# A vision block on one core: VectorE takes half of image 0's rotations, and the last steps get an order of their own

## What is computed

```python
h = wavelet_tokens(x, Wa, ba, Wd1, bd1, Wd2, bd2, Wd3, bd3)   # (32, 256, 256)
h = concatenate([cls_tok, h], axis=1)                          # 257 tokens
n = layernorm(h)
q, k, v = split(einsum('bsd,dhf->bshf', n, w_qkv) + b_qkv, 3)  # 16 heads of 64
q, k = q * cos + rotate_half(q) * sin, k * cos + rotate_half(k) * sin
s = q @ k.T / sqrt(192) + alibi, causal
h = h + softmax(s) @ v @ w_out + b_out
n = layernorm(h)                                               # feed-forward: 256 -> 1024 -> 256
h = h + bitlinear(silu(bitlinear(n, w_gate)) * bitlinear(n, w_up), w_down)
```

## Time and profile before

| | us |
|---|---|
| median of 3 runs (1750.04 to 1756.24) | 1754.96 |
| profiled execution | 1752.32 |
| its span, first to last instruction | 1750.50 |
| TensorE busy | 1664.2 |
| VectorE busy | 1470.0 |
| ScalarE busy | 1323.6 |
| POOL busy | 1120.1 |

### The profile page before, as it was taken

How to read it: one execution, slowest core, us unless ns; L and a number is a source line. 1 busy time by engine, 2 the same in 40 slices (tenths; PEclk the granted TensorE clock), 3 DMA queues, 4 the chain that set the end, 5 groups by cost and what they waited for, 6 DMA issues and landing times.

```text
span 1750.5 us, 48653 instructions
## 1 busy us (share of the span) xinstructions
PE 1664.2 (95%) x16742; PEld 1278.3 (73%) x16742; DVE 1470.0 (84%) x4972; ACT 1323.6 (76%) x3812; POOL 1120.1 (64%) x1034
## 2 busy tenths in 40 slices
PE   7758999999999999999999999999999999999975
PEld 6635777777777777777777777777777777777653
DVE  3837888899888888899888888899888888889874
ACT  0326888888888888888888888888888888888762
POOL 0087667766777666766777667666677667666500
PEclk9789999999999999999999999999999999999986
DMA  9311111111111111111111111111111111111100
GB/s 320 110 61 61 56 53 56 53 67 57 61 68 68 59 61 57 50 65 62 56 68 68 66 55 60 54 56 66 55 64 68 68 53 61 56 53 62 44 7 13
DMA packets 90168, 113.70 MB, mean 65 GB/s; under 512 B 14818, under 2 KB 52163, under 8 KB 89667
## 3 DMA queue, kind: packets, MB, share of 16 engines
q1 hardware_dynamic: 89922, 110.59, 18.1%
HBM read 26.62 MB, written 8.42 MB: 20 GB/s over the span
## 4 chain that ended last, share of the span: by engine, by line
PE 88%; DVE 4%; SPq 3%; POOL 2%; ACT 1%; issue 1%; DMA 0%; DVEq 0%; POOLq 0%; ACTq 0%
PE bank L725 45%; PE bank L842 9%; PE bank L983 7%; PE bank L831 6%; PE bank L829 6%; PE bank L994 3%; PE bank L853 3%; PE bank L903 3%; PE bank L891 2%; PE bank L1003 2%; SPq L320 1%; PE bank L882 1%; DVE arena L1283 1%; PE bank L950 0%; POOL rot L486 0%
## 5 line engine op out<-in xcount | busy, mean ns | idle before, releaser
L482 POOL TENSOR_TENSOR arena<-rq,cos 128x512 f32<-128x512 f32 x256 | 326.1, 1274 | 280.0 <-ACT rq L526 280.0
L535 ACT ACTIVATE arena<-arena,nm 128x129 f32<-128x129 f32 (+1 forms) x1024 | 455.6, 455 | 0.0
L486 POOL TENSOR_TENSOR rot<-rot,sin 128x512 f32<-128x512 f32 x256 | 326.3, 1275 | 103.9 <-DMA rot<-rq 103.9
L725 PE MATMUL bank<-xt_h,weights 128*128 128x256 f16 x2048 | 378.9, 273 | 9.2 <-ACT rq L526 7.8
L526 ACT ACTIVATE rq<-bank,bqk 128x256 f32<-128x256 f32 x512 | 214.4, 471 | 170.1 <-PE bank L725 155.3
L1283 DVE CUSTOM_DVE_ANT_0 arena<-bank,bias 128x129 f32<-128x129 f32 (+1 forms) x1024 | 317.9, 352 | 26.5 <-issue 16.6
L489 POOL TENSOR_TENSOR arena<-arena,rot 128x512 f32<-128x512 f32 x256 | 314.2, 1228 | 37.3 <-POOL rot L486 0.9
L1291 DVE TENSOR_TENSOR ptr_l<-bank,ptr_h 128x384 f16<-128x384 f32 x512 | 280.0, 552 | 31.8 <-ACT ptr_h L545 29.4
L545 ACT ACTIVATE ptr_h<-bank 128x384 f16<-128x384 f32 x512 | 249.1, 486 | 68.6 <-PE bank L725 44.0
L725 PE MATMUL bank<-xt_l,weights 128*128 128x256 f16 x1024 | 279.6, 273 | 0.0
L842 PE MATMUL bank<-eye,arena 128*128 128x128 f32 x1536 | 253.0, 277 | 8.5 <-DVE ptr_l L1291 4.4
(11 more groups left out here) (200 smaller groups left out, 3182.5 us busy)
## 6 DMA issues: line engine op xcount, KB each, us to landing
rot<-rq SPq DMA_DIRECT2D x512, 128.0 KB, 2.0
arena<-in_x SPq DMA_DIRECT2D x4, 2048.0 KB, 15.2
xin<-in_x SPq DMA_DIRECT2D x32, 256.0 KB, 2.8
hr<-hr SPq DMA_DIRECT2D x32, 256.0 KB, 2.3
out<-h SPq DMA_DIRECT2D x64, 128.0 KB, 2.1
arena<-in_L_attn_w_qkv SPq DMA_DIRECT2D x2, 1536.0 KB, 8.6
weights<-in_L_ffn_w_down SPq DMA_DIRECT2D x1, 1024.0 KB, 11.8
arena<-in_L_ffn_w_gate SPq DMA_DIRECT2D x1, 1024.0 KB, 8.5
```

What stands on the lines that cost most here:

```text
L482: pool.tensor_tensor(dst, rq[:, g % 2].rearrange("p j (t n) -> p j t n", t=T), cos[:, :].rearrange("p (t n) -> p t n", t=T).unsqueeze(1).b ...
L486: pool.tensor_tensor(r, r, sin[:, :].unsqueeze(1).broadcast_to([P, 2, SIDE]), ALU.mult).then_inc(t2_ready, 1)
L535: act.activation(cols, cols, ACT.Exp, bias=nm[:, t, h:h + 1], scale=-1.0, accum_out=rs[:, t, h:h + 1]).then_inc(e_done, 1)
L725: ins = pe.matmul(dst, lhs[l], rhs[r], start=start and n == 0, stop=stop and n == len(parts) - 1)
```

## The change

In the preparation, rotate(0, 1), rotate(0, 3), rotate(0, 5) and rotate(0, 7) go from POOL to VectorE, with waits that keep the three counters of the rotations in order. POOL does rotate(0, 0) ahead of add_bias(0). VectorE's image_operators(1, 16), image_out(1), image_stats(1), the split of wo_l and image_operators(17, 15) are placed between the rotations. The turns of the ternary weights go behind coarse(0) and between the first projections, on the banks 0, 1, 4 and 6, with their copies on ScalarE; the ternary steps of VectorE are spread accordingly. The mean of the weights is taken inside the last quarter of the gates' product. move(0) also waits until the weights are turned, because hr2 holds the third of them until then.

The loops end with step 29. Steps 30 to 33 (images 29 to 31 and the blocks up to 32) are written out call by call on each engine. The calls are the same; their order differs, on TensorE and ScalarE from step 30, on VectorE from the calls that go with it, on SP in the DMAs of these steps, and on POOL in one exchange, token_rstd(31) ahead of rotate(31, 7).

```diff
 # SP
+                if c == 0:
+                    sp.wait_ge(turned, 6)
 # POOL
-                if not image(b):
+                if not image(b) or begun and (b, g) == (0, 0) or b == 0 and g % 2:
                     return
+                if b == 0 and g:
+                    pool.wait_ge(pcos_done, g)
...
             pool.wait_ge(late_in, 16 * 13)
+            image_rstd(0)
+            rotate(0, 0)
 # ScalarE
+            coarse_out(0)
+            weights_out(0)
+            weights_out(1)
+            input_hi(0)
+            to_rotate(0, 0)
+            to_rotate(0, 1)
+            weights_out(2)
+            weights_out(3)
+            to_rotate(0, 2)
+            weights_out(4)
+            weights_out(5)
             act.wait_ge(rawo_in, 16)
             act.wait_ge(tern_ready, 3)
             act.activation(wo_h[:, :, :], rawo, ACT.Copy, scale=WSCALE).then_inc(w_hi, 1)
 # TensorE
             cls_part(psum[3], (2,), range(PAIRS))
+            pe.wait_ge(mean_ready, 1)
+            turn_weights(0)
             turn_input(0)
...
-            out_bias(range(0, 4))
             project(0, 0)
-            out_bias(range(4, PAIRS))
+            out_bias(range(PAIRS))
             pe.matmul(psum[2][:, 0:SIDE], ones[0:1, :], bo_row, start=False, stop=True).then_inc(ob_ready, 1)
+            project(0, 1)
+            turn_weights(1)
+            project(0, 2)
+            turn_weights(2)
 # VectorE
+            def rotate(b, g):
+                r = rot[:, g % 2].rearrange("p j (t n) -> p j t n", t=T)
+                dst = rope_out(b % 2, GROUPS[g])
+                dve.wait_ge(rq_ready, g + 1)
+                dve.wait_ge(pcos_done, g)
+                tt(dst, rq[:, g % 2]..., cos..., ALU.mult).then_inc(pcos_done, 1)
+                dve.wait_ge(rot_done[g % 2], 32 * (g // 2 + 1))
+                dve.wait_ge(t2_ready, g)
+                tt(rot[:, g % 2], rot[:, g % 2], sin..., ALU.mult).then_inc(t2_ready, 1)
+                dve.wait_ge(pcos_done, g + 1)
+                dve.wait_ge(t2_ready, g + 1)
+                dve.wait_ge(qk_done, g)
+                tt(dst, dst, r, ALU.add).then_inc(qk_done, 1)
...
             normalise_image(0)
-            dve.wait_ge(ops_ready, 1)
-            image_operators(1, 16)
+            ternary(1, 2)
             input_lo(0)
...
+            for part in range(3):
+                ternary(2, part)
+            prep_chain.settle()
+            rotate(0, 1)
             dve.wait_ge(ob_ready, 1)
             dve.tensor_copy(ob[:, :], psum[2][:, 0:SIDE]).then_inc(ob_copied, 1)
+            dve.wait_ge(ops_ready, 1)
+            image_operators(1, 16)
+            rotate(0, 3)
+            image_out(1)
+            image_stats(1)
+            rotate(0, 5)
+            dve.wait_ge(w_hi, 11)
+            stt(wo_l[:, :, :], rawo, WSCALE, wo_h[:, :, :], ALU.mult, ALU.subtract).then_inc(wo_split, 1)
+            rotate(0, 7)
             dve.wait_ge(ops_ready, 2)
             image_operators(17, 15)
```

More of the change, by code:

```diff
@@ L468, in image_rstd @@
             def image_rstd(a):
-                if not image(a):
+                if not image(a) or begun and a == 0:
                     return
@@ new lines, in _ @@
+            values(29, 2)
+            values(29, 3)
+            project(30, 4)
+            coarse(31)
+            synthesise(31)
+            scores(29, 4)
+            turn_tokens(29)
+            transposes(29, 6)
+            values(29, 4)
+            project(30, 5)
+            out_transposes(29, 0)
+            gate_up(29, 0)
+            project(30, 6)
+            values(29, 5)
+            transposes(29, 7)
+            scores(29, 5)
+            transposes(29, 8)
+            gate_up(29, 1)
@@ new lines, in _ @@
+            values(29, 6)
+            project(30, 7)
+            values(29, 7)
+            transposes(29, 9)
+            scores(29, 6)
+            project_v(30, 0)
+            gate_up(29, 2)
+            values(29, 8)
+            transposes(29, 10)
+            out_transposes(29, 1)
+            project_v(30, 1)
+            scores(29, 7)
+            values(29, 9)
+            transposes(29, 11)
+            project_v(30, 2)
+            turn_inner(29, 0)
+            transposes(29, 12)
@@ new lines, in _ @@
+            values(29, 10)
+            transposes(29, 13)
+            values(29, 11)
+            project_v(30, 3)
+            scores(30, 0)
+            gate_up(29, 3)
+            turn_input(31)
+            values(29, 12)
+            values(29, 13)
+            transposes(29, 14)
+            scores(30, 1)
+            out_transposes(29, 2)
+            project(31, 0)
+            down(29, 0)
+            transposes(29, 15)
+            project(31, 1)
+            values(29, 14)
+            transposes(30, 0)
@@ new lines, in _ @@
+            transposes(30, 5)
+            values(30, 3)
+            project(31, 4)
+            scores(30, 3)
+            project(31, 5)
+            turn_tokens(30)
+            scores(30, 4)
+            gate_up(30, 0)
+            values(30, 4)
+            transposes(30, 6)
+            out_transposes(30, 0)
+            scores(30, 5)
+            values(30, 5)
+            values(30, 6)
+            transposes(30, 7)
+            gate_up(30, 1)
+            transposes(30, 8)
+            project(31, 6)
@@ new lines, in _ @@
+            inner_peak(31, 3)
+            weights_lo(31, 13)
+            weights_lo(31, 14)
+            reciprocals(31, 3)
+            attended_lo(31, 2)
+            weights_lo(31, 15)
+            output(31, 0)
+            normalise(31, 3)
+            output(31, 1)
+            attended_lo(31, 3)
+            residual(32)
+            token_scales(32)
+            gate(32, 0)
+            gate_up(32, 0)
+            inner_peak(32, 0)
+            gate(32, 1)
+            gate_up(32, 1)
```

664 lines of the change are left out of this document (633 added, 31 removed).

## The result

| | us |
|---|---|
| before, median of 20 runs (1750.04 to 1756.24) | 1753.23 |
| after, median of 20 runs (1754.56 to 1758.85) | 1756.38 |
| ratio of after to before | 1.0019, interval 1.0012 to 1.0026 (95%) |
| profiled execution of after, its span | 1756.73, 1754.9 |

The time rose by 3.2 us. With so many runs that can be told from nothing, but it is well within the 0.5% that the prediction counts as no change. The total held. Its two large terms did not come out as written: the preparation costs 13 to 15 us and the last steps give back about 10.

A forecast was written before the change was run, and what follows sets the result against it. TensorE fills the steady step, so only start and end can move the time, the start through a chain of waits. Preparation +10.3 and last steps -8.4 give +1.9 on 1754.96, about 1757 us, range 1746 to 1768.

The forecast's parts named there:

- H: End of VectorE's hh in the preparation, 113.9 before; forecast 114.9 with port exclusion, 111.3 without; taken as +0.5 us.
- queue behind H: VectorE work queued ahead of values_lo(0,0), delaying the first value: floor +5.4, with port exclusion +9.65, taken as +8.5 us.
- lower clock behind coarse(1): TensorE idles about 9 us, then three value products run slower at the lower clock: 0 to +4, taken as +1.3 us.
- The exclusion: Preparation: VectorE instructions with two SBUF inputs and POOL's SBUF reads exclude one another; H +1.0 with it, -2.6 without.
- Move(0)'s new wait: Preparation: waiting for turned 6 costs nothing, since add_bias(0), which move(0) awaits too, ends later.
- Turn_tokens(30)'s and turn_inner(31,1)'s waits: Last steps: waits of 1.40 and 3.02 us, shortened by project(31,5) and by a maximum and rounding placed ahead: -1.3 and -3.0.
- The item of turn_tokens(31): Last steps, residual(31) to turn_tokens(31), waits of 2.29 and 1.48: token_scales passes weights_lo(31,4), giving -0.6 us.
- The last block: Block 32: inner_peak(32,2) and a scale, formerly behind gate_up(32,3) on the chain, now lie in a wait: -0.8 us.
- The short waits: Last steps: seven short waits of 5.6 us in all, giving back -1.5 us, a guess.
- the end of step 31: Two waits of 1.04 and 0.92 us, partly filled by project_v(31) stretched out later and scores(31) sooner: -1.2 us.
- the slower one: Port lockstep between H and values_lo(0,0), products at the lower clock: +14, only -3 from the end, 1766 us; chance 0.24.
- The faster one: POOL and VectorE hardly stop one another, or POOL's free time absorbs the late start: 1744.8 us or -8.4; together 0.16.

The follow-up runs named there:

- e4: Changed kernel with wo_l's split ahead of rotate(0,5) and image_operators(17,15) in two halves behind the second and third value products; 1750.43 us, ratio 0.9988 to before.
- e5: Changed kernel with cos and sin copied into a PSUM bank for VectorE's rotations, so eight of twelve instructions have one SBUF input; 1756.28 us, ratio 1.0030 to before.
- e9: Changed kernel plus 38 matmuls of 128x512, into a bank nobody reads, in the wait ahead of project_v(0,1); 1753.33 us, ratio 1.0003 to before.
- e2: Kernel before with its old preparation, but steps 30 to 33 written out as in the changed kernel; 1742.42 us, ratio 0.9949 to before.

## Why the prediction was right, step by step

**Right:** that no more than 0.5% changes, the time (1757 against 1756.4), the place of the loss and of the gain, and two of the rows named to show it: the first value 14.8 us later with image_operators and wo_l ahead of it, and VectorE's products at 1.09 to 1.75 us beside POOL. A third failed: turn_input(1) was to stand near 143, and stood at 148.84 and 148.37.

**The start, +10.3 against 13 to 15.** The terms, in the two traces of after, up to turn_input(1), beside the trace of before (its clock behind H was the higher one). The clock's row counts the lower level from coarse(1) on; that of the out_bias products ahead of it is in H's row, as in the prediction:

| | predicted | first trace | second trace |
|---|---|---|---|
| H, without the clock behind coarse(1) | +0.5 | +3.6 | +2.5 |
| queue behind H, without the clock | +8.5 | +8.0 | +8.5 |
| lower clock behind coarse(1) | +1.3 | +4.5 | +4.5 |
| sum | +10.3 | +16.1 | +15.5 |

The clock's row is 0.7 in the stretch from coarse(1) to H (5.4 us and not 4.7), 2.5 in the projections of the first trace (9.9 and not 7.4), and the rounds of the values, 1.3 and 3.8. The 2.5 is an upper bound: only group 5's projection, 2.76 us and not 1.50, lies on the chain of waits, and the first value is 1.9 further behind H than in the second trace; with 1.9 the first trace reads +8.5 and +3.9. Of the sum 1.4 and 0.4 us are given back by image 3, which the prediction didn't have. The ends that it gave, 0 and +14.6, just held what was left.

*H was mis-sized by 2 to 3 us.* Two steps of its chain failed. Project(0,0) began at 85.20 and not 83.4, 0.7 of it because all stood later already at the softmax. (The second trace began it at 86.31, but its out_bias took 3.78 us and not 5.31.) And rot of group 1 landed 4.6 us behind its rq (95.94 to 100.52), 3.9 in the second trace, where 2.75 was taken from an undisturbed pair in image 1. Why this landing is longer no run shows; group 2's swap is issued 2.5 us behind. The exclusion went the other way: it lengthened add_bias(0) by 1.44 us and the rotation and row operators by 1.1, where the upper end allowed 3.65. Move(0)'s new wait cost nothing, as written: its DMA is issued at 105.28, when add_bias(0) has ended.

*The queue* was sized right. Its upper reckoning (19.15 behind H, lockstep on every instruction) was near the 18.0 of the second trace. e4 shows that the queue is the place. e5, without the port in eight of the twelve products, still has 16.8 us behind H: most of the length is the order of wo_l, rotations and operators. How much of the rest is the port was not measured.

*The clock was mis-sized as much as H or more:* +1.3, with 4 as the bound, against 3.9 to 4.5. The step that failed is the one that gave the lower level to the value products alone, and there to about one round. One round is what the first trace has (+1.3), but it has the lower level between coarse(1) and H and in two projections too; in the second trace it lasts through all three rounds. e9 shows what it costs behind the wait where all three rounds have it: 4 us.

**The end, -8.4 against about -10.** From image 29's turn_input to the end before takes 243.1 us, after 233.4 and 232.3, e2 233.5: -9.7 to -10.8. Turn_tokens(30)'s and turn_inner(31,1)'s waits went as written. The item of turn_tokens(31) gave TensorE nothing: its waits of 2.29 and 1.48 became one of 3.79. The chain itself is shorter, as written: from residual(31) to turn_tokens(31) it takes 5.80 us (1683.67 to 1689.47) and not 6.26 (1673.48 to 1679.74), but about as much less of TensorE's own work lies inside it. The last block gained 1.2, where 0.8 was written. The short waits and the end of step 31, where the prediction guessed 2.7, hold the rest, 4 to 5; the windows above show TensorE with 0.4 us over up to 1665. Between the marks of images 29 and 31 the new order loses 0.9 us (98.9 against 98.1), which the prediction didn't have. It is small beside the spread and wasn't followed.

**What cancelled:** start and end were each taken too small, by some 3 to 4 and some 2 us. So the total is near by luck as well as by the reckoning. And 1757 was counted from a median of three runs, 1754.96, where 20 runs have 1753.23: the rise is 3.2 us and not 1.9.

The rivals: the slower one's mechanism was right as a mechanism (lockstep in that place, with products at the lower clock), and the start alone was as dear as it said. It didn't win because the end gave 10 and not 3. The faster one falls: the delay of the start is not taken up by POOL's free time ahead of image 1. That wait grew with the delay, from 5.87 to 19.47 us, and at image 3 the 16.0 us are still 14.6.

## What to carry to other kernels

Before work goes to an engine that looks idle, list what stands behind it in that engine's queue: here VectorE had 8 us free ahead of the values, and the twelve instructions cost more there than they saved on POOL. Sum a change that touches both ends of a program as two kernels, and run the two halves: some +14 and -10 looked like +3. And look for free time on the engine that is the bound (POOL ahead of add_bias and ahead of image 1) before taking its work away; two moves there, with the new end, gave 14 us.

## What the runs showed of the hardware

- The place of the lower TensorE clock in a start with many waits differs between executions of one program: two traces of the changed kernel have it in two projections and one round of the values, and in no projection and three rounds; 36 matmuls took 7.3 us at 1.00 and 11.1 at 0.52 behind the same order of calls.
- TensorE's clock stayed at the lower level through three rounds of six matmuls with waits of 1.42 us between them (granted 0.50 from 135.9 to 146.9 in the second trace of after); with 8.37 us of matmuls in the wait ahead of them the same rounds ran at 1.00 (134.0 to 145.0 in e9).
- A VectorE product of 128x512 with both inputs in SBUF takes 0.69 us, and up to 1.75 where it starts beside a running POOL instruction; with one input in PSUM it takes 0.68 there too. POOL's own product of that size goes from 1.27 to as much as 2.64 us (3.09 in the second trace) beside the split of wo_l.
